# The first gather by step, on a ring of 24 rows and without relays on SyncE

## What is computed

```python
agg = segment_sum(x[src], dst, num_segments=6250)      # the first gather
z   = (1 + eps) * x + agg
out = relu(batchnorm(relu(batchnorm(z @ W1 + b1)) @ W2 + b2 + x))
```

## Time and profile before

| | |
|---|---|
| median of 3 runs | 6660.27 us (6643.98 to 6661.23) |
| the profiled execution, span from first to last instruction | 7527.2 us |
| busy in the span | PE 5373.7, weight loads 3065.0, DVE 3160.7, ACT 545.2, POOL 4732.4 us |
| stage of the first gather | 58.7 to 1366 us |
| mean granted TensorE clock | 0.750 of full speed |

### The profile page before, as it was taken

One profiled execution on the slowest core, in us unless ns is written; L12 is line 12 of the kernel. 1 busy time (PEld: TensorE's weight loads), 2 busy tenths in 40 slices (PEclk: granted clock), 3 DMA queues, 4 the chain that ended last, 5 costly groups with the idle time before them and its releaser, 6 DMA issues. The chain is left out here.

```text
span 7527.2 us, 81611 instructions
## 1 busy us (share of the span) xinstructions
PE 5373.7 (71%) x17807; PEld 3065.0 (41%) x17807; DVE 3160.7 (42%) x6956; ACT 545.2 (7%) x1542; POOL 4732.4 (63%) x4778
## 2 busy tenths in 40 slices
PE   5666777638765556636566687788888888888887
PEld 2333333525332223324444575433433344444444
DVE  2222444528655556674444567511111123333317
ACT  0000000324000000010000001100000000000004
POOL 5666665664666666677677404766666666666665
PEclk8777777969767777767778899865555588888869
DMA  4444433331688888846667675433333333333445
GB/s 137 133 134 130 124 123 121 128 100 66 214 256 256 265 262 268 266 134 210 210 217 226 205 191 148 126 89 89 90 89 87 89 111 119 119 119 119 123 101 191
DMA packets 693161, 1164.20 MB, mean 155 GB/s; under 512 B 104128, under 2 KB 490285, under 8 KB 692614
## 3 DMA queue, kind: packets, MB, share of 16 engines
q0 software_dynamic: 224288, 633.55, 28.9%
q1 hardware_dynamic: 468344, 525.21, 21.9%
q10 hardware_dynamic: 110, 0.23, 0.0%
HBM read 870.83 MB, written 287.77 MB: 154 GB/s over the span
## 5 line engine op out<-in xcount | busy, mean ns | idle before, releaser
L2126 PE MATMUL l_sums<-big 128*128 (+1 forms) x3520 | 1701.9, 578 | 349.1 <-issue 135.1
L195 DVE TENSOR_TENSOR big<-iota_row,dst_tab 128x512 f32<-128x512 f32 x660 | 458.4, 695 | 2171.3 <-PE l_sums L2126 712.1
L1280 POOL DMA_INDIRECT bin_rows<-staging,place_tab x832 | 979.6, 1177 | 337.4 <-issue 249.1
L1166 POOL DMA_INDIRECT big<-kv_rows,idx_tab x880 | 832.0, 945 | 503.0 <-issue 241.1
L578 POOL DMA_INDIRECT big<-in_x,big x832 | 826.6, 994 | 483.6 <-SPq L148 237.7
L2083 POOL DMA_INDIRECT big<-x_rows,place_tab x880 | 882.3, 1003 | 394.9 <-issue 241.7
L2083 POOL DMA_INDIRECT big<-x_rows,idx_tab x832 | 817.2, 982 | 426.7 <-issue 226.6
L1220 PE MATMUL es_q<-big 128*128 x1760 | 720.9, 536 | 450.3 <-issue 343.3
L2126 PEld LDWEIGHTS l_sums<-big 128*128 128x128 f32 x3520 | 765.2, 259 | 502.0 <-issue 473.7
L612 PE MATMUL l_sums<-big 128*128 x1760 | 723.0, 543 | 331.9 <-issue 235.8
L1504 PE MATMUL ws_sums<-big 128*128 128x264 f32 x1760 | 546.1, 474 | 321.2 <-DVE big L1524 170.9
(11 more groups left out here) (297 smaller groups left out, 5187.4 us busy)
## 6 DMA issues: line engine op xcount, KB each, us to landing
v_edge<-big SPq DMA_DIRECT2D x880, 128.0 KB
big<-v_edge SPq DMA_DIRECT2D x220, 512.0 KB
bin_rows<-big SPq DMA_DIRECT2D x110, 520.0 KB
sims<-bin_rows SPq DMA_DIRECT2D x110, 520.0 KB
staging<-in_edges SPq DMA_DIRECT2D x104, 520.0 KB
gate_rows<-big SPq DMA_DIRECT2D x49, 512.0 KB
big<-gate_rows SPq DMA_DIRECT2D x49, 512.0 KB
big<-kv_rows,idx_tab POOLq DMA_INDIRECT x880
```

What stands on the lines that cost most here:

```text
L195: return dve.tensor_tensor(out, rows, columns.unsqueeze(2).to_broadcast([P, QUAD, P]), ALU.is_equal)
L1166: pool.indirect_dma_start(ring[:, u, :], None, k.kv_rows, bass.IndirectOffsetOnAxis(ap=k.idx[:, s:s + 1], axis=0)).then_inc(s_row[u], 16)
L1280: pool.indirect_dma_start(k.bin_rows, bass.IndirectOffsetOnAxis(ap=k.place[:, c:c + 1], axis=0), k.staging[:, g % 2, j, :], None).then_inc ...
L2126: pe.matmul(sums[:, bank_of(node[u] + turn, D)], onehot[:, u % HALF, :], flat[:, bass.ds(at, D)], start=False, stop=True, skip_group_check ...
```

## The change

- The gather goes by step: 880 gathers with the columns of `k.idx`. The table of sources by chunk (`by_chunk`, `src_c`) and its load are gone.
- The ring has 24 places with 24 semaphores of its own. PE waits for the row's semaphore against a constant and reads at a fixed place. POOL waits every four gathers for PE's count of steps.
- SP relays nothing. It issues fill q when step 8q is done.
- 16 one-hots instead of 8; comparisons are made 8 steps ahead instead of 4.
- The edge sort: 6 places for marks instead of 2, 4 for bases instead of 2, ranks in 4 PSUM banks instead of 2, and a place is read 13 steps after its mark is begun instead of 5. The fill's source lies in `k.staging`, the places in `k.binning`.
- DVE doesn't wait for SP's releases before `finish`.

```diff
@@ step_tables
-            sp.dma_start(k.by_chunk, k.src_cols).then_inc(s_x, 16)
-            sp.wait_ge(s_x, 64)
+            sp.wait_ge(s_x, 48)
@@ bin_positions
+BIN_HOTS = 6
+BIN_WIDE = 4
-    hot = room.take([P, 2, OCT, NW], BF16)
+    hot = room.take([P, BIN_HOTS, OCT, NW], BF16)
-    fill = room.take([P, OCT, ER])
+    fill = k.staging[:, 0, :, :]
-    wide = room.take([NW, 2, OCT, NW])
+    wide = room.take([NW, BIN_WIDE, OCT, NW])
+    ranks = spread + [counts[:, h, :] for h in range(2)]
...
-            if g >= 2:
-                pe.wait_ge(s_taken, 2 * g - 2)
-            out = spread[g % 2]
+            if g >= len(ranks):
+                pe.wait_ge(s_taken, 2 * (g - len(ranks)) + 1)
+            out = ranks[g % len(ranks)]
...
-                if g >= 2:
-                    dve.wait_ge(s_spread, g - 1)
-            elif g >= 2:
-                dve.wait_ge(s_counted, g - 1)
+                if g >= BIN_HOTS:
+                    dve.wait_ge(s_spread, g - BIN_HOTS + 1)
+                    dve.wait_ge(s_taken, 2 * (g - BIN_HOTS) + 1)
+            elif g >= BIN_HOTS:
+                dve.wait_ge(s_counted, g - BIN_HOTS + 1)
...
-            if PLACE_AT + 5 <= s < PLACE_AT + 5 + 4 * OCTS and s % 4 == 1:
-                place((s - PLACE_AT - 5) // 4)
+            if PLACE_AT + 13 <= s < PLACE_AT + 13 + 4 * OCTS and s % 4 == 1:
+                place((s - PLACE_AT - 13) // 4)
@@ first_gather
+FIRST_RING = 24
+FIRST_HOTS = 16
+FIRST_LEAD = 8
-        ring = room.take([P, U, D + 1])
-        onehot = room.take([P, HALF, P])
+        ring = room.take([P, FIRST_RING, D + 1])
+        onehot = room.take([P, FIRST_HOTS, P])
+        s_row = sems(nc, k, *(f"l0_row{n}" for n in range(FIRST_RING)))
...
-            for c in range(NC):
-                u = c % U
-                if u % QUAD == 0 and c >= U:
-
-                    pool.wait_ge(s_used, c + QUAD - U)
+            for s in range(STEPS):
+                u = s % FIRST_RING
+                if u % QUAD == 0 and s >= FIRST_RING:
+
+                    pool.wait_ge(s_sum, s + QUAD - FIRST_RING + 1)
                 pool.indirect_dma_start(ring[:, u, 0:D], None, table, bass.IndirectOffsetOnAxis(
-                    ap=k.by_chunk[:, c:c + 1], axis=0)).then_inc(s_row[u], 16)
+                    ap=k.idx[:, s:s + 1], axis=0)).then_inc(s_row[u], 16)
...
-            sp.sem_inc(s_here, HERE)
-            lasts = None
-            for c in range(NC):
-                lasts = relay_chunk(nc, sp, lasts, k.lasts, c, s_row, row0, s_here, s_sum, s_used)
-                if c % OCT == 5:
-                    work.fill(sp, c // OCT)
-            for q in range(OCTS, BIN_OCTS):
+            for q in range(BIN_OCTS):
+                sp.wait_ge(s_sum, q * OCT + 1)
                 work.fill(sp, q)
...
-                chunk_ready(pe, s, node[u], s_here)
+                pe.wait_ge(s_row[s % FIRST_RING], 16 * (s // FIRST_RING + 1))
...
-                pe.matmul(sums[:, bank_of(node[u], width)], onehot[:, u % HALF, :],
-                          flat[:, bass.ds(slot_of(s, node[u], D + 1), width)],
+                pe.matmul(sums[:, bank_of(node[u], width)], onehot[:, s % FIRST_HOTS, :],
+                          ring[:, s % FIRST_RING, 0:width],
...
-                if s >= HALF:
-                    dve.wait_ge(s_sum, s + QUAD - HALF + 1)
+                if s >= FIRST_HOTS:
+                    dve.wait_ge(s_sum, s + QUAD - FIRST_HOTS + 1)
...
-                if s % QUAD == 0 and s + QUAD < STEPS:
-                    hot(s + QUAD)
+                if s % QUAD == 0 and s + FIRST_LEAD < STEPS:
+                    hot(s + FIRST_LEAD)
...
-            dve.wait_ge(s_used, NC - BEHIND)
             work.finish(dve)
```

More of the change, by code:

```diff
@@ L370, in bin_positions @@
     taken = room.take([P, OCT, NW])
-    fill = room.take([P, OCT, ER])
-    places = room.take([P, NC])
-    wide = room.take([NW, 2, OCT, NW])
+    fill = k.staging[:, 0, :, :]
+    wide = room.take([NW, BIN_WIDE, OCT, NW])
     room = k.binning
@@ L379, in bin_positions @@
     base = upto
-    full = room.take([NW, NC])
+    places = room.take([P, NC])
+    full = places[0:NW, :]
     begun = room.take([NW - 1, ROWS])
@@ L410, in count_bins @@
                 c = g * OCT + j
-                ins = pe.matmul(counts[0:NW, c * 2 // NC, c % (NC // 2):c % (NC // 2) + 1], hot[:, g % 2, j, :],
+                ins = pe.matmul(counts[0:NW, c * 2 // NC, c % (NC // 2):c % (NC // 2) + 1], hot[:, g % BIN_HOTS, j, :],
                                 ones[:, 0:1], start=True, stop=True)
@@ L431, in rank @@
                 pe.wait_ge(s_line, 12)
-            if g >= 2:
-                pe.wait_ge(s_taken, 2 * g - 2)
-            out = spread[g % 2]
-            pe.matmul(out[:, 0:OCT * NW], above, hot[:, g % 2, :, :].rearrange("p r w -> p (r w)"), start=True, stop=False)
+            if g >= len(ranks):
+                pe.wait_ge(s_taken, 2 * (g - len(ranks)) + 1)
+            out = ranks[g % len(ranks)]
+            pe.matmul(out[:, 0:OCT * NW], above, hot[:, g % BIN_HOTS, :, :].rearrange("p r w -> p (r w)"), start=True, stop=False)
             pe.wait_ge(s_wide, g + 1)
-            pe.matmul(out[:, 0:OCT * NW], k.ones[0:NW, :], wide[:, g % 2, :, :].rearrange("v r w -> v (r w)"),
+            pe.matmul(out[:, 0:OCT * NW], k.ones[0:NW, :], wide[:, g % BIN_WIDE, :, :].rearrange("v r w -> v (r w)"),
                       start=False, stop=True).then_inc(s_spread, 1)
@@ L467, in mark @@
                 dve.wait_ge(s_line, 8)
-                if g >= 2:
-                    dve.wait_ge(s_spread, g - 1)
-            elif g >= 2:
-                dve.wait_ge(s_counted, g - 1)
-            dve.tensor_tensor(hot[:, g % 2, :, :], k.iota_row[:, 0:NW].unsqueeze(1).to_broadcast([P, OCT, NW]),
+                if g >= BIN_HOTS:
[3 more added lines that the diff above has]
+                dve.wait_ge(s_counted, g - BIN_HOTS + 1)
+            dve.tensor_tensor(hot[:, g % BIN_HOTS, :, :], k.iota_row[:, 0:NW].unsqueeze(1).to_broadcast([P, OCT, NW]),
                               bin_f[:, g * OCT:(g + 1) * OCT].unsqueeze(2).to_broadcast([P, OCT, NW]),
@@ L476, in widen @@
         def widen(g):
-            if g >= 2:
-                dve.wait_ge(s_spread, g - 1)
-            dve.tensor_tensor(wide[:, g % 2, :, :], k.ident[0:NW, 0:NW].unsqueeze(1).to_broadcast([NW, OCT, NW]),
+            if g >= BIN_WIDE:
+                dve.wait_ge(s_spread, g - BIN_WIDE + 1)
+            dve.tensor_tensor(wide[:, g % BIN_WIDE, :, :], k.ident[0:NW, 0:NW].unsqueeze(1).to_broadcast([NW, OCT, NW]),
                               base[:, g * OCT:(g + 1) * OCT].unsqueeze(2).to_broadcast([NW, OCT, NW]),
@@ L487, in place @@
             dve.wait_ge(s_taken, 2 * g)
-            dve.tensor_tensor(taken.rearrange("p r w -> p (r w)"), spread[g % 2][:, 0:OCT * NW],
-                              hot[:, g % 2, :, :].rearrange("p r w -> p (r w)"), ALU.mult).then_inc(s_taken, 1)
+            dve.tensor_tensor(taken.rearrange("p r w -> p (r w)"), ranks[g % len(ranks)][:, 0:OCT * NW],
+                              hot[:, g % BIN_HOTS, :, :].rearrange("p r w -> p (r w)"), ALU.mult).then_inc(s_taken, 1)
             dve.wait_ge(s_taken, 2 * g + 1)
@@ L557, in first_gather @@
         room = Arena(k.side)
-        room.take([P, NC], I32)
-        ring = room.take([P, U, D + 1])
-        flat = ring.rearrange("p u d -> p (u d)")
-        onehot = room.take([P, HALF, P])
+        ring = room.take([P, FIRST_RING, D + 1])
+        onehot = room.take([P, FIRST_HOTS, P])
         zeros = room.take([1, BANK])
         sums = psum(nc, ctx, "l0_sums", [P, BANKS * BANK])
[L564 to L567, removed]
+        s_zero, s_hot, s_sum, s_taken, s_free = sems(nc, k, *(f"l0_{n}" for n in (
+            "zero", "hot", "sum", "taken", "free")))
+        s_row = sems(nc, k, *(f"l0_row{n}" for n in range(FIRST_RING)))
         work = bin_positions(nc, k, ctx, room)
@@ L619, in hot @@
             def hot(s):
-                if s >= HALF:
-                    dve.wait_ge(s_sum, s + QUAD - HALF + 1)
-                compare(dve, k, onehot[:, s % HALF:s % HALF + QUAD, :], None, k.dst[:, s:s + QUAD]).then_inc(s_hot, QUAD)
+                if s >= FIRST_HOTS:
+                    dve.wait_ge(s_sum, s + QUAD - FIRST_HOTS + 1)
+                at = s % FIRST_HOTS
+                compare(dve, k, onehot[:, at:at + QUAD, :], None, k.dst[:, s:s + QUAD]).then_inc(s_hot, QUAD)
             dve.memset(ring[:, :, D:D + 1], 1.0).then_inc(s_zero, 1)
             dve.memset(zeros[:, :], 0.0).then_inc(s_zero, 1)
-            hot(0)
+            for s in range(0, FIRST_LEAD, QUAD):
+                hot(s)
             beside = work.vector(dve)
             for s in range(STEPS):
-                if s % QUAD == 0 and s + QUAD < STEPS:
-                    hot(s + QUAD)
+                if s % QUAD == 0 and s + FIRST_LEAD < STEPS:
+                    hot(s + FIRST_LEAD)
                 beside(s)
```

(2 more changed lines are left out.)

## The result

The changed kernel takes 6699 us in the median (6693 to 6722), the one before 6658 us (6644 to 6661) beside it: ratio 1.0074, 95% interval 1.0053 to 1.0095. It is 0.7% slower, where 0.6% faster was forecast.

What follows compares the result with a forecast made beforehand. POOL's gather pace plus waits for SP's relays was taken to bound the first gather stage: -213 + 62 + 15 - 5 = -141 us profiled; with half the waits real, -42 us, 6618 us, range 6515 to 6710.

Steps and rivals of the forecast that it cites:

- w = 0.5: Share of the first gather stage's profiled waits taken to exist in timed runs; gave -42 us, 6618 us.
- the stage's 213 us of waiting: POOL's waits in the first gather's stage, all laid to SP's relayed release; to go in the profiled execution.
- The formula with w = 0: Gain for the whole kernel, 198w - 57 us; if timed runs have none of the waits, +57 us, 6717 us.
- The signs that the prediction named: In the changed profile: no L148 waits, stage 1150 to 1170 us, PE register work about 0.1 us, tail under 9.
- two readings that exclude each other: Of the first gather stage's waits: none in timed runs (w = 0, 6717 us) or all (w = 1, 6519 us).
- The rival on the other side: First gather stage: relays cost nothing when not profiled, 48 more gathers are pure cost; +57 us, 6717 us; chance 0.25.
- Pace: POOL in the first gather's stage: 1.30 us a gather, so 48 more gathers cost +62 us.
- What stays as waits: POOL's waits left in the changed first gather stage: bounded by 0 and 155 us, taken as 15 us.
- The ring: First gather's ring: old length enough for a landing of about 2.4 us; larger one pays only for PE stalls, 26 us.
- The end of the stage: Behind the first gather stage's last gather: last fill goes out earlier, leaving some 8 us; -5 us.
- PE as the bound of the second half: Rival, first gather stage: at low clock PE needs 5.9 us a group against POOL's 5.2; +73 us, 6691; chance 0.13.
- DVE beside the gathers: First gather stage: a two-port rule would put 1.7 us per four gathers on POOL's path; taken not to move the difference.

Runs made afterwards that it cites:

- experiment 1: The kernel before, unchanged, run again for the second profile (span 6664.2 us): 6662.6 us, ratio 1.0001.
- The disturbed execution: The profiled execution of the kernel before from which the prediction was made, also called the first: span 7527 us, against a median of 6660.
- experiment 6: The changed kernel with SP's relays put back, still 880 gathers by step on a ring of 24: 6706.5 us, ratio to the kernel before 1.0075.
- experiment 3: The kernel before with 48 gathers more, into a scratch row that nobody reads: 6719.9 us, ratio 1.0084.
- experiment 2: The changed kernel with 48 of its 880 gathers left out: 6649.6 us, ratio to the kernel before 0.998.
- experiment 7: The changed kernel on a ring of 16 with 8 one-hots made 4 steps ahead: 6703.6 us, ratio to the kernel before 1.0068.
- Experiment 4: The kernel before, by chunk with relays on the ring of 16, with the rest of the change and last fills issued early: 6657.1 us, ratio 0.9991.

## Why the prediction was wrong

- **The step that failed is the choice of w = 0.5**, the share of the stage's 213 us of waiting that the timed runs have, and that the change would give back. It is 0. The prediction had the row that said so: the time outside the gathers plus 3424 gathers at 1.25 us came to the median exactly. It was set aside because PE and DMA seemed too busy for it. The second profile shows what both sides of that sum really are: 4424 us of gathers with their gaps (1.29 each) and 2240 us of the rest. So the agreement to the microsecond was partly luck, but its meaning, that POOL waits nowhere, was right. The formula with w = 0 gives +57 us; +41 to +49 were measured, and +49.7 in the stage. The signs that the prediction named came: a stage of 1149.4 us (1150 to 1170 was named), no waits of POOL, PE's register work at 0.103 us at most, 6.8 us behind the last gather, and a span that fell where the median didn't, which it had called w near 0.
- **The disturbed execution was taken for the kernel.** A profiled span 13% above the median is the warning, and the text saw it; it then took the middle of two readings that exclude each other. Experiments 1 and 6 show that the relays cost nothing, with PE's register work at 128 ns and under.
- **The rival on the other side was right** in mechanism and price: relays that only have to keep ahead of a landing cost nothing, and 48 gathers are pure cost. Its reason was too wide: the relay has 6.5 us for a landing and not 12 rows. It had 0.25 and deserved most of the chance.
- **Pace.** 1.30 us a gather was right (1.304 and 1.298), and +62 us for 48 gathers was right (61.6 and 62.9 in the stages of experiments 3 and 2). In the change itself it is 57.2, since its gathers were 6 ns shorter on average.
- **What stays as waits** was put at 15 us and is 0. The comparison with the second turn of the last gathers misled: its 83.8 us of waiting belonged to the same disturbance. In the second profile that group has 243.5 us of issue gaps, and its other 24.7 us are pieces of 0.30 us too.
- **The ring.** That the old length was enough was right (experiment 7), and the larger one paid for stalls that don't exist. The landing was put too low: 2.4 us were read from one gather and the operation behind it, and the estimate from the Trainium skill's page "DMA: Bandwidth & Descriptors" (section "Anatomy of one DMA — SWDGE (gpsimd) path") was 2.3. The traces have 2.7 us at least and 2.8 in the median, and that decides.
- **The end of the stage** was put at -5 us; it is -7.5 (14.3 to 6.8). Experiment 4 gets 4.6 of it with relays (14.3 to 9.7), by spreading the fills.
- **PE as the bound of the second half** didn't come: POOL waits for nothing in either half. The sum of the stage leaves no room for it.
- **DVE beside the gathers.** The changed kernel's gathers average 994 ns over a median of 946, those of before 1000 over 947, with the same work of DVE: what DVE costs them can be at most those 50 ns. The prediction took a rule on two-port operations for these, and they aren't such. The Trainium skill's page "SBUF — State Buffer", section "Who interferes with whom", says that `tensor_tensor` has no 2-port mode and that `tensor_reduce` never contends on trn2; comparison, mark, base and both halves of a place are these two. The trace agrees: nothing of the 1.7 us for four gathers that the prediction worked out shows.

What stays open is what disturbed the first execution. Its PE and SP sequencers were held up to 1.4 us at single register or semaphore instructions, PE's only in the stages with relays; but the second turn of the last gathers, without relays, lost 139 us as well. No later profile had PE's register work held so, with relays or without, so it couldn't be tried. Whether the profiler had a part isn't shown either way.

## What to carry to other kernels

Before a wait in a profile is worth anything, set the profiled span against the median: here nine of ten profiles lay within 0.3% of their kernel's median, and the one that misled lay 13% above. Where they differ, take a second profile, or trust sums that can be made from counts and paces alone. Where one engine issues a fixed number of equal operations back to back, the number is the time: a change that spared its helpers' work and added 6% to the number of its gathers made them 5% longer from first to last (1085 to 1142.5 us). And an engine that only passes semaphores on was free here, with 6.5 us between the issue of a gather and the moment when its landing is needed. That distance has to be worked out from the waits, not taken from the ring's length. The same 6.5 us, with a landing and PE's step to fit in, cost 24 us of the stage on the ring of 8.

## What the runs showed of the hardware

- An indirect gather of 128 rows of 1 KB takes 0.946 us of POOL in the median, and 0.30 us pass before the next one; that pace (1.30 us with the slower ones) didn't depend on the relays or on a ring of 16 or 24.
- Its landing comes 2.8 us after the start of its issue in the median, 2.7 at the earliest (5.4 and 4.8 at the latest in the two kernels).
- With rows of 2 KB, in the edge scores, POOL's part is the same (0.947 us), and the landing takes longer: 4.9 us in the median (3.5 to 6.3, L1166 in the second profile of before).
- An undisturbed profiled execution of this kernel takes as long as its other runs (a span of 6691.7 us, runs of 6693 to 6722), so a profile need not cost time. What cost the first one its 867 us isn't shown.
